# Mixer: the gate product of every turn on GpSimd behind the output weights, the skip on VectorE

## The reference, cut to what matters

```
proj = x @ in_proj_w.T                     # gate | hBC | dt
hBC  = silu(causal conv of 4 taps(hBC))    # -> hs, B, C
A_cum = cumsum(dt * A)
Y    = ((C B^T) * exp(min(A_cum_l - A_cum_s, 0)) * mask) @ (hs * dt)  + hs * D     # the skip
g    = Y * silu(gate)                      # the gate product
out  = (g * rsqrt(mean over the group of g^2 + eps) * norm_w) @ out_proj_w.T
```

## Time and profile before

| | |
|---|---|
| runs of the kernel before | 2897.49, 2899.88, 2897.47 us; median 2897.49 |
| the profiled execution | 2899.4 us, of which the span from first to last instruction is 2897.7 us |
| busy in the span | PE 2592.7 us (89%), DVE 1862.7 (64%), ACT 1366.3 (47%), POOL 1144.2 (39%) |
| the mixer's groups | from about 367 us to 1830 us of the span, eight periods of some 184 us |
| in a group, turn after turn (392 to 576 us) | PE 173.4, DVE 144.3, POOL 108.3, ACT 103.9 us busy of 184.0 |

### The profile page before, as it was taken

One profiled execution on the slowest core, in us unless ns is written; L12 is line 12 of the kernel. 1 busy time (PEld: TensorE's weight loads), 2 busy tenths in 40 slices (PEclk: granted clock), 3 DMA queues, 4 the chain that ended last, 5 costly groups with the idle time before them and its releaser, 6 DMA issues. The chain is left out here.

```text
span 2897.7 us, 43385 instructions
## 1 busy us (share of the span) xinstructions
PE 2592.7 (89%) x14384; PEld 2110.6 (73%) x14384; DVE 1862.7 (64%) x2991; ACT 1366.3 (47%) x2581; POOL 1144.2 (39%) x901
## 2 busy tenths in 40 slices
PE   7877499999999999999999998699999999999958
PEld 4435377777777777777777876588888888888846
DVE  4554389597795976968769697354644645546453
ACT  2221266465554654646546464354544544545431
POOL 3000156475564755646556565222122222221210
PEclk9888799999999999999999999799999999999989
DMA  3000232031230312303223030101001000010010
GB/s 139 1 0 1 69 109 103 34 125 58 81 128 34 121 62 81 116 17 131 80 77 110 26 131 23 58 23 30 18 22 29 18 22 22 22 29 18 11 51 30
DMA packets 62131, 163.75 MB, mean 57 GB/s; under 512 B 8400, under 2 KB 9040, under 8 KB 53520
## 3 DMA queue, kind: packets, MB, share of 16 engines
q1 hardware_dynamic: 59808, 158.14, 16.2%
q10 hardware_dynamic: 2160, 3.43, 0.3%
HBM read 158.92 MB, written 2.62 MB: 56 GB/s over the span
## 5 line engine op out<-in xcount | busy, mean ns | idle before, releaser
L157 PE MATMUL bank<-XH,d_w_hi 128*128 128x512 f32 x1160 | 472.0, 407 | 31.6 <-POOL d_w_lo L1111 18.0
L159 PE MATMUL bank<-XH,d_w_lo 128*128 128x512 f32 x1160 | 458.3, 395 | 4.6 <-issue 4.6
L158 PE MATMUL bank<-XL,d_w_hi 128*128 128x512 f32 x1160 | 456.0, 393 | 0.0
L1111 POOL TENSOR_TENSOR d_w_lo<-d_w,d_w_hi 128x512 fp32r<-128x512 f32 x144 | 224.0, 1556 | 325.5 <-ACT d_w_hi L996 325.3
L1214 DVE SCALAR_TENSOR_TENSOR d_hs<-bank,d_conv,d_hs 128x508 f32<-128x508 f32 (+2 forms) x384 | 279.5, 740 | 47.6 <-ACT d_hs L1017 38.6
L157 PEld LDWEIGHTS bank<-XH,d_w_hi 128*128 128x128 f32 x1160 | 219.8, 190 | 89.3 <-issue 25.1
L1136 POOL TENSOR_TENSOR d_decay<-d_decay,d_acg 128x1024 f32<-128x1024 f32 x128 | 270.3, 2131 | 0.0
L159 PEld LDWEIGHTS bank<-XH,d_w_lo 128*128 128x128 f32 x1160 | 219.6, 189 | 56.4 <-issue 6.8
L158 PEld LDWEIGHTS bank<-XL,d_w_hi 128*128 128x128 f32 x1160 | 220.3, 190 | 43.8
L1141 POOL TENSOR_TENSOR d_gated_lo<-d_gated,d_gated_hi 128x512 fp32r<-128x512 f32 x128 | 165.6, 1297 | 205.3 <-ACT d_gated_hi L1045 205.3
L1247 DVE TENSOR_TENSOR d_decay<-d_decay,d_cb 128x1024 f32<-128x1024 f32 x128 | 181.3, 1456 | 76.4 <-ACT d_decay L1037 76.4
(11 more groups left out here) (280 smaller groups left out, 6586.3 us busy)
## 6 DMA issues: line engine op xcount, KB each, us to landing
d_decay<-running_sums SPq DMA_DIRECT2D x64, 1024.0 KB, 4.8
d_w<-in_L_w_groups SPq DMA_DIRECT2D x144, 256.0 KB, 3.4
e_w<-in_L_w_heads SPq DMA_DIRECT2D x80, 256.0 KB, 2.6
d_wo<-in_L_wo_groups SPq DMA_DIRECT2D x64, 256.0 KB, 4.9
X<-in_x SPq DMA_DIRECT2D x8, 256.0 KB, 10.6
b_ctx<-in_ctx SPq DMA_DIRECT2D x8, 256.0 KB, 11.7
e_ctx<-in_ctx SPq DMA_DIRECT2D x8, 256.0 KB, 2.7
out<-X SPq DMA_DIRECT2D x8, 256.0 KB, 2.0
```

The lines of the kernel that those rows point to most:

```text
L157: pe.matmul(out, wh, xh, start=first, stop=False)
L158: pe.matmul(out, wh, xl, start=False, stop=False)
L159: return pe.matmul(out, wl, xh, start=False, stop=last)
L1111: pool.tensor_tensor(WL[:, w, :, :], WR[:, w, :, :], WH[:, w, :, :].bitcast(F32), ALU.subtract).then_inc(q["w_split"], 1)
```

## The change

The gate product leaves VectorE's queue. What is left there is called `skip`, with the same waits in front of turn 0. GpSimd gets a `gated` of its own: for each half it waits for the skip and for ScalarE's gate, and multiplies. It stands at the end of each iteration, behind the output weights; the product of turn 7 stands between `w_lo(g+1, 1)` and `w_lo(g+1, 2)`, and in the last group in front of `gated_lo`. The semaphores and what waits for them stay as they are.

```
+                def gated(g, j):
+                    for h in range(2):
+                        n = 2 * (g * JT + j) + h
+                        gt = GT[:, j, tokens(h)]
+                        pool.wait_ge(q["skip"], START + n + 1)
+                        pool.wait_ge(q["gate"], START + n + 1)
+                        pool.tensor_tensor(gt, gt, GATE[:, j % 2, tokens(h)], ALU.mult).then_inc(q["gated"], 1)
+
...
                         for k in WO_AFTER.get(j + 1, ()):
                             wo(g, k)
+                        gated(g, j)
                     if not last_group:
                         w_lo(g + 1, 1)
+                        gated(g, JT - 1)
                         w_lo(g + 1, 2)
                         diff(g + 1, 0)
                         w_lo(g + 1, 3)
+                    else:
+                        gated(g, JT - 1)
                     gated_lo(g, 0)
...
-                def gated(g, j):
+                def skip(g, j):
...
                         v.scalar_tensor_tensor(gt, HS[:, j % 2, tokens(h)], PD[:, j:j + 1], c.bank[2 + h][:, :],
                                                ALU.mult, ALU.add).then_inc(q["skip"], 1)
-                        v.wait_ge(q["skip"], START + n + 1)
-                        v.wait_ge(q["gate"], START + n + 1)
-                        v.tensor_tensor(gt, gt, GATE[:, j % 2, tokens(h)], ALU.mult).then_inc(q["gated"], 1)
...
                         clamp(g, j + 1)
-                        gated(g, j)
+                        skip(g, j)
                         xdt(g, j + 1)
...
                         conv(g + 1, 0)
-                    gated(g, JT - 1)
+                    skip(g, JT - 1)
```

## The result

The changed kernel takes 2950.96 us at the median of four runs (2950.0 to 2952.6) against 2898.04 of the kernel before: 1.0184 times as long, 95% interval 1.0171 to 1.0197. It is slower by 53 us. 2971.5 was forecast, 20 us too much, inside the range of 2918 to 2996. The profiled execution has 2950.0 us, span 2948.3, so the sum of +74 is to be held against +50.6.

A forecast was written before the change was run, and what follows sets the result against it. VectorE was taken to bound turns before, GpSimd with its holds after. Seven groups with borders at 9.0 us (63), the last group 5 and the clock 6 made +74 on 2899.4; less 1.9, 2971.5 us, range 2918 to 2996.

The forecast's parts named there:

- What bounds a turn: Late turns of a group: VectorE sets the pace of 14.57 us; TensorE's own is 14.01.
- The holds: VectorE and GpSimd share an exclusive lock for a whole instruction; the waiting engine gets it before the holder's next.
- Rival 1: Engines don't exclude one another for the product, only the border counts: about 2896 us, no change; chance 0.10.
- Part 2: GpSimd gets two products of 1.25 us each turn; its queue with holds sums to 15.35 us and bounds the turn.
- the scan of turn 2: In each group, the next project after this scan comes 1.25 us later, products and scores taking turns before w_lo.
- the prediction's largest term: Turns 3 to 6 at GpSimd's pace: turn 3 +0.3 us, turns 4 to 6 +2.35 us a group.
- Turn 7: From T, the start of project(g, 17), w_lo(g+1, 1) ends at T + 18.35 instead of 16.51: +1.9 us.
- The border: Between groups, turn 7's product waits for skip before w_lo(g+1, 2); TensorE waits 4.4 us, gate ends +3.2 us later.
- Part 5: Longer TensorE idles at the borders bring the low clock more often: about 0.9 us a border, from nothing to 2.
- Rival 2: Holds fall partly into gaps: turns near 14.57, turns 2 and 7 lose 0.5 each, border 3.2; about 2928 us; chance 0.14.
- Rival 3: No exclusion, and the border is hidden because turn 7's skip comes before the tile is wanted: 2876 us; chance 0.04.
- Rival 4: The product on GpSimd costs as much as the dearest hold, 2.07 us instead of 1.25: about 3050 us; chance 0.06.

The follow-up runs named there:

- no_product: Kernel before with the gate product cut to one column on VectorE (gate left out of the result): 2866.8 us, ratio 0.9879.
- scores_psum_before: Kernel before with the scores' second operand from PSUM instead of SBUF (mask and C B^T left out of the result): 2874.7 us, ratio 0.991.
- scores_psum_after: Changed kernel with the scores' second operand from PSUM instead of SBUF (mask and C B^T left out of the result): 2900.1 us, ratio 1.0003.
- border_late: Changed kernel with the product of turn 7 moved behind w_lo(g+1, 3) in GpSimd's queue: 2917.3 us, ratio 1.0076 to the kernel before.
- turns_only: Changed kernel with only the product of turn 7 put back on VectorE: 2919.4 us, ratio 1.0074 to the kernel before.
- border_only: Changed kernel with the products of turns 0 to 6 put back on VectorE: 2931.2 us, ratio 1.0111 to the kernel before.
- both_off: Changed kernel with turn 7's product behind w_lo(g+1, 3) and the scores' second operand from PSUM (mask and C B^T left out): 2862.3 us, ratio 0.988.
- before_w_lo_waits: Kernel before with one more wait: GpSimd's w_lo(g, 5+2j) waits for both halves of scores(g, j): 2902.1 us, ratio 1.0007.

## Why the prediction was right, and where it was off

**What bounds a turn** was read rightly: VectorE's 14.57 over TensorE's 14.01. no_product and scores_psum_before both land on 14.0 (turns 4 to 6).

**The holds** (the part on overlaps) were the right mechanism, and they decided the case: without the scores' holds the changed kernel is at 2900. **Rival 1** fell on that in the turns, where it had the scores at 1.2 us beside a running product. Its world, and nearly its number (2896), is the scores_psum_after experiment, 2900.

**The size of a hold was the term that failed.** Part 2 took a hold as long as the VectorE instruction that causes it, 1.2 us for half of the scores and 0.6 for half a clamp. They hold for 0.98 and 0.45: the "whole instruction" of the prediction is too long by 0.2 us when it is read off the recorded length. In the cycle of 15.35 us that is 2 x 0.22 + 2 x 0.15 = 0.74 too much, and 14.61 is within 0.06 of the measured 14.67. The rows for it were in front of me: `diff` held for 2.89 - 1.92 = 0.97 us and the scaling for 1.49 - 1.04 = 0.45. I took the length of the one that holds, where the one that is held says how long it stood. The error comes back in each turn: turns 3 to 6 were to lose 2.65 a group and lost 0.25, the scan of turn 2 0.9 instead of 1.25. GpSimd with what it waits for is the bound of a turn all the same, but only 0.1 us above the pace of before. So the loss does not come from the prediction's largest term: turns 3 to 6 were to bring 21 us in eight groups and brought 2. Turns 2 and 7 and the border carried it.

**Turn 7** lost 1.1 us instead of 1.9, and this is the same error once more. In the changed kernel `w_lo(g+1, 1)` is done at T + 17.5 in all seven groups, not at T + 18.35; where the clock stays up (five groups of border_late, one of turns_only) the next `project` starts at T + 17.64, that is +1.13 over the 16.51 of the earlier trace rows, and 1.9 - 0.74 is 1.16. The changed kernel's own 17.98 to 18.35 come from the scan, which ran in part at the low clock at all seven borders (0.50 to 0.64 in its stretch); before, it did at four of seven, where the stretch took 17.2 to 17.6. The clock adds 0.5 us to the mean of both kernels. That three groups show just the forecast 18.35 is chance.

**The border** was right in its cause and size: `project(g+1, 2)` started 9.3 us after `project(g+1, 1)` (9.3 to 9.6 over the seven borders) where +9.9 was forecast, because skip h0 was done at +5.3, and the cost was 4.4 us where 3.2 and a clock term of 0.9 were. border_only, where the scan runs at full clock at six of seven borders, has skip h0 at +6.0, `project(g+1, 2)` at +9.96 and a wait of 4.2 us there, where +6.0, +9.9 and 4.4 were forecast. By its time the border costs 32 us in all; the sum had 29.

Three things at the border came otherwise. TensorE's wait, though, shows as 2.0 us and not 4.4 in the group shown above, and as 2.9 to 3.9 at the other six: the scan and the first matmuls of `project(g+1, 1)` ran in part at the lower clock and so took up some of it. The last link was another than forecast: `out` found ScalarE's gate done 0.3 us earlier at all seven borders and waited for nothing; TensorE's own queue, late by the wait, ended last. And the clock fell more often, as Part 5 says: beside the scans, it fell behind the wait at five of seven borders, where the way from `project(g+1, 2)` to `out` took 15.5 us instead of 13.9.

**Rival 2** had the turns near 14.57 and 2928 us. The turns did come out near that, but turns 2 and 7 and the border cost more than it allowed. **Rival 3** was wrong for this kernel; both_off (2862, its number was 2876) is its world, and shows that it lacked two things, the absence of holds and another place in the queue, not an earlier skip. **Rival 4** was wrong: the product takes 1.30 us at the median, and up to 2.29 only where it is held.

## What to carry to other kernels

Before an elementwise step moves to GpSimd, look at what VectorE runs at that moment: if that instruction reads two operands from SBUF, as the scores do, the two don't overlap, and the moved step costs its own length and the neighbour's hold. (The clamp, with one operand in SBUF, held GpSimd too, for 0.45 us.) Price a hold by the row of the instruction that is held (its length less its length alone), never by the one that holds. And look at what stands behind a new wait in an in-order queue: here the same product, behind `w_lo`, `diff` and `w_lo` instead of in front of them, was worth 34 us.

## What was not expected of the hardware

The same instructions settled into two paces. In the kernel before, seven groups ran turns 4 to 6 at 14.56 us and one at 14.00, and the difference that I see in the rows is the moment at which `w_lo` arrived, 0.8 or 1.5 us after the start of the scores, with a gap on VectorE in front of them (0.46 us in the row above) that the other pace doesn't have, and with clamps held for longer (2.81 us for two instead of 2.58). In border_only two other groups ran at 14.00. In both, the scan of turn 2 had come later than usual (after 16.8 to 16.9 us instead of 16.3). In all three the pace, once set in, kept up until turn 6. What sets it in is not shown, and before_w_lo_waits, which forced `w_lo` behind the scores, did not bring it about. So a pace read in one group may not be that of the next.
